# Pair layers: key copies and stores by context and own tokens, second unit's loads on ScalarE's queue

## The chip, the cores and the metric

One core of one Trainium2 chip. The metric is the device time of the whole program in microseconds, as the median of several executions.

## The reference, cut to what matters

Four attention layers run one after the other on x (4 batches of 256 tokens, 256 channels) with a context of the same shape. Layer 0 is a cross attention of two halves with an MLP, layer 2 a wide grouped attention. The change touches layers 1 and 3 alone, the pair layers:

```python
h = jnp.concatenate([x, latents], axis=1)               # x: the context, latents: the own tokens
q = (latents @ q_w + q_b).reshape(b, k_len, NH, DH)     # 16 heads of 16
kv = (h @ kv_w + kv_b).reshape(b, p + k_len, NH, DH, 2)
kmat, v = (kv[..., 0], kv[..., 1])
attn = jnp.einsum('bkhd,bnhd->bhkn', q, kmat) / DH      # 256 queries on 512 keys
attn = jnp.where(full_mask[:, None, None, :], attn, -jnp.inf)
attn = jax.nn.softmax(attn.astype(jnp.float32), axis=-1).astype(q.dtype)
attn_out = jnp.einsum('bhkn,bnhd->bkhd', attn, v).reshape(b, k_len, H)
```

The output projection, a norm and an MLP follow.

## The kernel before

The program is a row of stages. Each stage is a block in which SyncE, GpSimd, TensorE, ScalarE and VectorE run their own instruction lists, tied by semaphores, and ends with a barrier of all five. A pair layer (`pair_layer`, L2637) has three: projections (`pair_projections`, L1685, for layer 1; `scale_and_projections`, L2490, for layer 3, which first finishes layer 2), attention (`pair_attention`, L2048), and `project_and_mlp`.

**Projections.** Products are made from high and low float32r parts, three matmuls for one. `PairWork` lists 12 groups, each 128 output rows by 512 tokens, two batches: (is_k, m, src, half), where m is the block of eight heads (0, the *early* block, or 1, the *late* one), src 0 the context tokens and src 1 the own tokens. In both layers the order of the early block is: groups 0 and 1 context keys, 2 and 3 own keys, 4 and 5 queries. The late block follows as groups 6 to 11. For each group TensorE multiplies (`group`, L1630), ScalarE writes the high part with the bias (`high`, L1664), and VectorE writes the low part (`low`, L1669), which raises `qk_lo`. A PSUM bank is used again four groups later. Groups that read own tokens need their transposes (`turn`, L1623) split into parts by ScalarE and VectorE (`turned_high`, `turned_low`); groups of context keys read the context's parts, which lie ready. In layer 1 all four transposes come ahead of group 0. In layer 3 groups 0 and 1, then four tiles of values, come ahead of the transposes. Last come the values (`values`, `add_values`).

**Stacked operands.** The attention multiplies stacks of 48 rows, three sets of 16 for one head: (key high, query low), (key high, query high), (key low, query high). Row 48 holds the mask on the key side and ones on the query side; row 49 holds ones on the key side and the negated maxima on the query side. The 16 heads form four units of four heads; a unit's stacks lie in one of three slots. Since rows move between partitions, the stacks are filled by DMA:

- `fill_rows` (L1575): SyncE issues the six constant rows and waits for all.
- `copy_first_unit` (L1591): SyncE waits until `qk_lo` is 4 (`first_k`, both halves of the keys), issues 12 key copies, three for each head j, waits until it is 6 (`first_q`), issues 12 query copies, then waits for all 24 (`c.UNIT` is 24*16) and for the four stores. The stage can't end before that.
- `store_second_unit` (L1602): ScalarE, between `high` 7 and `high` 8, issues four DMAs which write the second unit's half of the early block to DRAM (`k_second`, `q_second`).

A key copy (L1520) moves 16 partitions with 8 KB each, a query copy (L1524) 16 partitions with 4 KB each:

```python
eng.dma_start(k_st[rows, a].bitcast(F32).rearrange("d b n -> d (b n)"),
              self.k[(0, 0, 1)[n]][at:at + c.HD].bitcast(F32).rearrange("d b s t -> d (b s t)")
```

**Attention.** There are 16 quads (unit, batch). A round works on the scores of one quad (`S`), the maxima of the one before (`M`), the shifted, transposed scores and exponentials of the one before that (`E`), and the value products of the next older one (`P`, `X`); the order on each engine is the text at L2056 to L2058. In a round SyncE waits for the negated maxima (`mx_out`) of a quad and issues two DMAs that put them into row 49 (L2115); the first `E` step of the next round waits for them (`row_in`, L2208). Behind them on the same queue: in rounds 0 and 1 (`first in (0, 1)`) the second unit's six key and six query loads from DRAM (`SecondUnit.load`, L1541), in rounds 2 to 5 the third unit's copies from the late block, six a round, in rounds 7 to 10 those of the fourth. The second unit is needed from round 4 on.

Of the kernel before, what the change touches and what calls it, by code (L numbers as in the profile page):

```python
# [5 lines left out]
P = 128  # L6
# [1497 lines left out]
class HeadParts:  # L1504
# [6 lines left out]

    def load_head(self, c, eng, g, j, q_st, k_st, sem, kinds="kq"):


        a, half = divmod(j, 2)
        at = (4 * (g % 2) + j) * c.HD
        for n in range(3):
            rows = slice(half * c.HALF + n * c.HD, half * c.HALF + (n + 1) * c.HD)
            if "k" in kinds:
                eng.dma_start(k_st[rows, a].bitcast(F32).rearrange("d b n -> d (b n)"),  # L1520
                              self.k[(0, 0, 1)[n]][at:at + c.HD].bitcast(F32).rearrange("d b s t -> d (b s t)")
                              ).then_inc(sem, 16)
            if "q" in kinds:
                eng.dma_start(q_st[rows, a].bitcast(F32).rearrange("d b t -> d (b t)"),  # L1524
                              self.q[(1, 0, 0)[n]][at:at + c.HD].bitcast(F32)).then_inc(sem, 16)


class SecondUnit:
# [6 lines left out]
    def store(self, eng, parts, sem):  # L1535
        for part in range(2):
            eng.dma_start(self.k[part], parts.k[part][P // 2:P].bitcast(F32).rearrange("c b s t -> c (b s t)")
                          ).then_inc(sem, 16)
            eng.dma_start(self.q[part], parts.q[part][P // 2:P].bitcast(F32)).then_inc(sem, 16)
# [12 lines left out]
class PairWork:  # L1552
# [4 lines left out]
    def __init__(self, st, core, c, late, second_unit, q_st, k_st, v_st, z, turned, qk_ps, groups):  # L1557
# [9 lines left out]
        self.tiles = [(src, b) for src in range(2) for b in range(B)]  # L1567
        self.first_k = max(n for n, g in enumerate(groups) if g[0] and not g[1]) + 1
# [22 lines left out]
    def copy_first_unit(self, sp):  # L1591
        c, z = self.c, self.z
        sp.wait_ge(z.qk_lo, self.first_k)
        for j in range(4):
            self.early.load_head(c, sp, 0, j, self.q_st[:, 0], self.k_st[:, 0], z.first_in, "k")
        sp.wait_ge(z.qk_lo, self.first_q)
        for j in range(4):
            self.early.load_head(c, sp, 0, j, self.q_st[:, 0], self.k_st[:, 0], z.first_in, "q")
        sp.wait_ge(z.first_in, c.UNIT)
        sp.wait_ge(z.stored, 4 * 16)  # L1600

    def store_second_unit(self, act):  # L1602
        act.wait_ge(self.z.qk_lo, self.first_q)
        self.second_unit.store(act, self.early, self.z.stored)
# [80 lines left out]
def pair_projections(core, c, late, second_unit, q_st, k_st, v_st):  # L1685

    with core.stage(f"p{c.layer}") as st:
# [6 lines left out]
        with core.nc.Block() as block:  # L1694
# [11 lines left out]
            def _(pe):  # L1706
                for n in range(4):
                    work.turn(pe, n)
                for g in range(len(groups)):
                    work.group(pe, g)  # L1710
# [4 lines left out]
            @block.scalar  # L1715
            def _(act):
                for n in range(4):
                    work.turned_high(act, n)
                for g in range(len(groups)):
                    if g == work.first_q + 2:  # L1720
                        work.store_second_unit(act)
                    work.high(act, g)

            @block.vector
            def _(dve):
                for n in range(4):
                    work.turned_low(dve, n)
                for g in range(len(groups)):
# [319 lines left out]
def pair_attention(core, c, weights, a_tok, late, second_unit, o_all, q_st, k_st, v_st):  # L2048
# [22 lines left out]
    with core.stage(f"s{L}") as st:  # L2071
# [15 lines left out]
        with nc.Block() as block:  # L2087
# [8 lines left out]
            def _(sp):  # L2096
# [12 lines left out]
                def body(first, second, third, fourth):  # L2109
# [8 lines left out]
                    if first in (0, 1):  # L2118
                        second_unit.load(c, sp, first == 0, slots[1][first == 0], unit_in[0])
# [14 lines left out]
            def _(act):  # L2134
                def body(first, second, third, fourth):
                    for kind, n in act_steps:
# [6 lines left out]
                        elif kind == "O" and fourth is not None:  # L2143
                            act.wait_ge(z.o_done, fourth + 1)
                            wait(act, z.x_done, fourth)
                            nc.scalar.activation(oT[:], o_ps, ACT.Copy).then_inc(z.o_out, 1)
                rounds(body)
# [342 lines left out]
def scale_and_projections(core, shared, before, c, gamma, beta, late, second_unit, q_st, k_st, v_st):  # L2490

    nc, ins, x, HT = core.nc, core.ins, core.x, TT // 2
    with core.stage(f"p{c.layer}") as st:
# [12 lines left out]
        with nc.Block() as block:  # L2506
# [39 lines left out]
            def _(act):  # L2546
# [17 lines left out]
                for g in range(2, len(groups)):  # L2564
                    if g == work.first_q + 2:
                        work.store_second_unit(act)
# [136 lines left out]
```

## Time and profile before

| | |
|---|---|
| median of 3 runs | 1305.93 us (1305.92 to 1308.3) |
| the profiled execution's own time | 1308.49 us |
| its span, first to last instruction | 1306.7 us |
| TensorE busy | 1211.3 us, 93% of the span |
| VectorE busy | 968.6 us, 74% |
| ScalarE busy | 736.1 us, 56% |
| GpSimd busy | 507.3 us, 39% |
| mean granted TensorE clock | 0.958 |
| projections of layer 1, attention of layer 1 begins | 714.20, 749.83 us |
| projections of layer 3, attention of layer 3 begins | 1071 (with layer 2's last part), 1124.18 us |

Times in the rows are microseconds from the span's start; a row gives start, duration, engine, line, operation, output<-inputs, shapes, a count where equal neighbours are merged, and in brackets how long the engine had been idle and what ended it. PE is TensorE, DVE VectorE, ACT ScalarE, SPq and ACTq the DMA issues of SyncE's and ScalarE's queues (their duration is that of the issue, not of the transfer). A release by PEq with the line of a stage's block is the barrier between two stages.

### The profile page before, as it was taken

The page shows a single profiled execution, that of the slowest core. Times are in us where ns is not written, and L with a number is a line of the kernel's source. Part 1 is how long each engine was busy: PE and PEld are TensorE (multiplying, and loading weights), DVE is VectorE, ACT ScalarE, POOL GpSimd, SP SyncE. Part 2 cuts the span into 40 slices and gives each one's busy share as a digit, 9 for nine tenths or more (in the row PEclk, how much of TensorE's full clock was granted, in tenths as well). Part 3 has the DMA queues.
Part 4 walks back from the last instruction along what each step waited for, and adds up shares of the span by engine and source line. Part 5 has one row for each costly group of instructions (what it writes and reads, how often), then busy time and mean ns, then how long its engine had stood idle before and what let it go on. Part 6 is the DMA issues. An engine that isn't in the chain of part 4 may idle for free. (4 is left out here: it accounts for less than half of the span.)

```text
span 1306.7 us, 27356 instructions
## 1 busy us (share of the span) xinstructions
PE 1211.3 (93%) x9144; PEld 1000.9 (77%) x9144; DVE 968.6 (74%) x2179; ACT 736.1 (56%) x1670; POOL 507.3 (39%) x670
## 2 busy tenths in 40 slices
PE   5999999999799999999889879999899999499989
PEld 4999999999699999999769735558677778255578
DVE  5878787887788788778785468947488876589474
ACT  5665655766466656567662237764166664077651
POOL 4645455444474454554041000122299970001040
PEclk9999999999899999999989959999999999589899
DMA  5210011010211101110030697220384003876021
GB/s 176 58 34 15 27 32 32 24 32 1 101 34 34 33 9 32 32 32 8 1 101 2 129 106 87 41 83 25 89 197 85 2 10 72 127 81 83 2 69 33
DMA packets 56534, 70.90 MB, mean 54 GB/s; under 512 B 6864, under 2 KB 47572, under 8 KB 54104
## 3 DMA queue, kind: packets, MB, share of 16 engines
q1 hardware_dynamic: 54832, 65.83, 24.7%
q10 hardware_dynamic: 1600, 3.76, 1.0%
q8 instruction: 57, 0.93, 0.3%
q14 instruction: 45, 0.37, 0.1%
HBM read 46.79 MB, written 8.13 MB: 42 GB/s over the span
## 5 line engine op out<-in xcount | busy, mean ns | idle before, releaser
L932 ACT ACTIVATE a_prob<-a_s_ps,a_negmax 128x257 f32<-128x257 f32 x256 | 119.0, 476 | 92.8 <-DVE a_negmax L1014 92.8
L2156 DVE TENSOR_REDUCE s_mx<-s_s_ps 128x2 f32<-128x1024 f32 x128 | 152.0, 1211 | 18.3 <-PE s_s_ps L2201 17.9
L2141 ACT ACTIVATE s_probT<-s_st_ps 128x512 f32<-128x512 f32 x256 | 132.2, 606 | 57.7 <-PE s_st_ps L2215 55.4
L873 POOL TENSOR_TENSOR x_v_hi<-a_v_sum,x_one 128x512 fp32r<-128x512 f32 x60 | 63.2, 1054 | 243.8 <-DVE a_v_sum L1003 243.8
L1938 POOL TENSOR_SCALAR s_below<-s_masked,s_mx 128x256 f32<-128x256 f32 x256 | 117.8, 480 | 4.0 <-DVE s_mx L1966 3.1
L1029 DVE TENSOR_TENSOR a_pT_lo<-a_t_ps,a_pT_hi 128x512 fp32r<-128x512 f32 x128 | 88.2, 689 | 37.2 <-ACT a_pT_hi L945 35.5
L1014 DVE TENSOR_REDUCE a_negmax<-a_s_ps 128x2 f32<-128x514 f32 x128 | 86.8, 688 | 23.0 <-PE a_s_ps L1075 22.9
L945 ACT ACTIVATE a_pT_hi<-a_t_ps 128x512 fp32r<-128x512 f32 x128 | 76.7, 599 | 46.7 <-PE a_t_ps L1129 43.1
L2278 POOL TENSOR_TENSOR a_k_high<-x_tok,parts_b_out 128x256 f32<-128x256 f32 x16 | 11.1, 731 | 229.3 <-DMA parts_b_out<-L_xattn_out_b 229.3
L1966 DVE CUSTOM_DVE_ANT_0 s_masked<-s_s_ps,l_mask 128x256 f32<-128x256 f32 x256 | 90.7, 420 | 4.5 <-PE s_s_ps L2003 4.5
L2201 PE MATMUL s_s_ps<-l_k_st,l_q_st 49*128 49x512 f32 x192 | 68.1, 546 | 22.2 <-PEq L2506 10.2
L1951 ACT ACTIVATE s_probT<-s_st_ps 128x512 f32<-128x512 f32 x128 | 69.7, 595 | 29.1 <-PE s_st_ps L2013 29.0
L1073 PE MATMUL a_s_ps<-x_k_hi,x_q_hi 128*128 128x258 f32 x256 | 74.5, 291 | 10.7 <-ACT a_prob L932 5.4
L948 ACT ACTIVATE a_oT_hi<-a_o_ps,a_hc 128x256 fp32r<-128x256 f32 x128 | 60.7, 474 | 37.0 <-PE a_o_ps L1075 29.7
L1073 PE MATMUL a_o_ps<-a_pT_hi,x_v_hi 128*128 128x256 f32 x256 | 81.1, 317 | 0.0
L1129 PE MATMUL a_t_ps<-ident,a_prob 128*128 128x128 f32 x512 | 77.2, 273 | 3.1 <-ACT a_prob L940 2.0
L2215 PE MATMUL s_st_ps<-l_q_st,l_k_st 50*128 50x256 f32 x384 | 70.0, 338 | 10.7 <-DMA l_q_st<-s_mxT 10.6
L875 POOL TENSOR_TENSOR x_v_lo<-a_v_sum,x_v_hi 128x512 fp32r<-128x512 f32 x60 | 77.4, 1290 | 4.7
L2215 PEld LDWEIGHTS s_st_ps<-l_q_st,l_k_st 50*128 50x128 f32 x384 | 48.3, 204 | 33.1 <-DMA l_q_st<-s_mxT 12.9
L1075 PE MATMUL a_s_ps<-x_k_hi,x_q_lo 128*128 128x258 f32 x256 | 72.6, 284 | 0.0
L1075 PE MATMUL a_g_ps<-a_wo_hi,a_oT_lo 128*128 128x256 f32 x256 | 72.6, 284 | 0.0
L1074 PE MATMUL a_s_ps<-x_k_lo,x_q_hi 128*128 128x258 f32 x256 | 72.6, 283 | 0.0
(348 smaller groups left out, 4039.3 us busy)
## 6 DMA issues: line engine op xcount, KB each, us to landing
a_wo_raw<-L_xattn_wo SPq DMA_DIRECT2D x16, 256.0 KB, 3.3
x_wqk_raw<-L_xattn_wq SPq DMA_DIRECT2D x31, 128.0 KB, 2.3
x_wqk_raw<-L_xattn_wk SPq DMA_DIRECT2D x31, 128.0 KB, 2.3
x_wv_raw<-L_xattn_wv SPq DMA_DIRECT2D x15, 256.0 KB, 3.1
l_k_st<-k_second SPq DMA_DIRECT2D x12, 256.0 KB, 9.8
l_k_st<-k_stack SPq DMA_DIRECT2D x16, 192.0 KB
l_q_st<-q_stack SPq DMA_DIRECT2D x12, 192.0 KB
x_vbias<-L_xattn_bias_v SPq DMA_DIRECT2D x2, 1024.0 KB, 6.5
```

Source lines behind the costliest of these rows:

```text
L875: nc.gpsimd.tensor_tensor(lo, raw, hi.bitcast(F32), ALU.subtract).then_inc(z.v_split, 1)
L932: nc.scalar.activation(prob[:, n % 2, qt, 0:NK], s_ps[:, n % 2, qt, 0:NK], ACT.Exp, bias=negmax[:, n % 2, qt:qt + 1], accum_out=den[:, n % ...
L1014: nc.vector.tensor_reduce(negmax[:, n % 2], s_ps[:, n % 2, :, 0:NK], AX.X, ALU.max, negate=True).then_inc(z.max_done, 1)
L1029: nc.vector.tensor_tensor(pT_lo[:, n % 2], t_ps[:], pT_hi[:, n % 2].bitcast(F32), ALU.subtract).then_inc(z.t_out, 1)
L1073: nc.tensor.matmul(out, a_hi, b_hi, start=start, stop=False)
L1075: return nc.tensor.matmul(out, a_lo, b_hi, start=False, stop=stop)
L1129: mm = nc.tensor.transpose(t_ps[:, at:at + P], prob[:, n % 2, qt, kt * P:(kt + 1) * P], core.ident[:])
L1938: nc.gpsimd.tensor_scalar(below[:, i % 2, h, qt], masked[:, i % 2, h, qt], -1.0, mx[:, i % 2, h, qt:qt + 1], ALU.mult, ALU.add).then_inc(z ...
L1966: nc.vector.tensor_tensor_reduce(out=masked[:, i % 2, h, qt], in0=s_ps[:, h, qt], in1=mask[:, i // NQ * QT + qt], scale=1.0, scalar=-3.0e3 ...
L2141: nc.scalar.activation(probT[:, third % 2, n // 4, n // 2 % 2, n % 2], st_ps[:, u % 3], ACT.Exp, scale=c.scale).then_inc(z.exp_done, 1)
L2156: nc.vector.tensor_reduce(mx[:, i % 2, qt, a::2], s_ps[:, n % 2], AX.X, ALU.max).then_inc(z.max_done, 1)
L2215: mm = nc.tensor.matmul(st_ps[:, u % 3, j * S:(j + 1) * S], k[:, a, kt * P:(kt + 1) * P], q[:, a], start=True, stop=True)
```

## The change

1. `copy_first_unit` copies keys by halves: when `qk_lo` is 2 (`context_k`) the context's 12 pieces (`load_key_half`: 16 partitions, four runs of 1 KB each), when it is 4 the own tokens' 12; queries as before; 36 DMAs for 24.
2. `store_second_unit` is called before each `high` and issues the context keys' two stores before `high` 4, the own keys' before `high` 6, the queries' before `high` 8; six DMAs for four.
3. In layer 1 groups 0 and 1 (and their `high` and `low`) go ahead of the transposes, as they do in layer 3.
4. The second unit's 12 loads are issued by ScalarE ahead of its first attention round, and no longer by SyncE in rounds 0 and 1.

```diff
--- before.py
+++ after.py
@@ -1509,6 +1509,15 @@
         self.k = [k_high if k_high and part == "hi" else st.sb(f"{name}_k_{part}", [P, B, 2, S], F32R)
                   for part in ("hi", "lo")]
 
+    def load_key_half(self, c, eng, j, src, k_st, sem):
+
+        a, half = divmod(j, 2)
+        tokens = slice(src * S, (src + 1) * S)
+        for n in range(3):
+            rows = slice(half * c.HALF + n * c.HD, half * c.HALF + (n + 1) * c.HD)
+            eng.dma_start(k_st[rows, a, :, tokens].bitcast(F32),
+                          self.k[(0, 0, 1)[n]][j * c.HD:(j + 1) * c.HD, :, src, :].bitcast(F32)).then_inc(sem, 16)
+
     def load_head(self, c, eng, g, j, q_st, k_st, sem, kinds="kq"):
 
 
@@ -1532,10 +1541,13 @@
         self.q = core.nc.dram_tensor(f"q_second{c.layer}", (2, P // 2, T), F32).ap()
         self.k = core.nc.dram_tensor(f"k_second{c.layer}", (2, P // 2, B * c.NK), F32).ap()
 
-    def store(self, eng, parts, sem):
+    def store_keys(self, eng, parts, src, sem):
         for part in range(2):
-            eng.dma_start(self.k[part], parts.k[part][P // 2:P].bitcast(F32).rearrange("c b s t -> c (b s t)")
-                          ).then_inc(sem, 16)
+            eng.dma_start(self.k[part].rearrange("c (b s t) -> c b s t", s=2, t=S)[:, :, src, :],
+                          parts.k[part][P // 2:P, :, src, :].bitcast(F32)).then_inc(sem, 16)
+
+    def store_queries(self, eng, parts, sem):
+        for part in range(2):
             eng.dma_start(self.q[part], parts.q[part][P // 2:P].bitcast(F32)).then_inc(sem, 16)
 
     def load(self, c, eng, is_k, dst, sem):
@@ -1565,6 +1577,7 @@
         self.bq, self.bk = columns(core, f"L{L}_xattn_q_b"), columns(core, f"L{L}_xattn_kv_b")
         self.chunks = [(kt, slice(half * 512, (half + 1) * 512)) for half in range(2) for kt in range(KT)]
         self.tiles = [(src, b) for src in range(2) for b in range(B)]
+        self.context_k = max(n for n, g in enumerate(groups) if g[0] and not g[1] and not g[2]) + 1
         self.first_k = max(n for n, g in enumerate(groups) if g[0] and not g[1]) + 1
         self.first_q = max(n for n, g in enumerate(groups) if not g[0] and not g[1]) + 1
 
@@ -1590,18 +1603,24 @@
 
     def copy_first_unit(self, sp):
         c, z = self.c, self.z
-        sp.wait_ge(z.qk_lo, self.first_k)
-        for j in range(4):
-            self.early.load_head(c, sp, 0, j, self.q_st[:, 0], self.k_st[:, 0], z.first_in, "k")
+        for src, count in enumerate((self.context_k, self.first_k)):
+            sp.wait_ge(z.qk_lo, count)
+            for j in range(4):
+                self.early.load_key_half(c, sp, j, src, self.k_st[:, 0], z.first_in)
         sp.wait_ge(z.qk_lo, self.first_q)
         for j in range(4):
             self.early.load_head(c, sp, 0, j, self.q_st[:, 0], self.k_st[:, 0], z.first_in, "q")
-        sp.wait_ge(z.first_in, c.UNIT)
-        sp.wait_ge(z.stored, 4 * 16)
-
-    def store_second_unit(self, act):
-        act.wait_ge(self.z.qk_lo, self.first_q)
-        self.second_unit.store(act, self.early, self.z.stored)
+        sp.wait_ge(z.first_in, 36 * 16)
+        sp.wait_ge(z.stored, 6 * 16)
+
+    def store_second_unit(self, act, g):
+        for src, count in enumerate((self.context_k, self.first_k)):
+            if g == count + 2:
+                act.wait_ge(self.z.qk_lo, count)
+                self.second_unit.store_keys(act, self.early, src, self.z.stored)
+        if g == self.first_q + 2:
+            act.wait_ge(self.z.qk_lo, self.first_q)
+            self.second_unit.store_queries(act, self.early, self.z.stored)
 
     def place(self, part, g):
         is_k, m, src, half = self.groups[g]
@@ -1704,9 +1723,11 @@
 
             @block.tensor
             def _(pe):
+                for g in range(2):
+                    work.group(pe, g)
                 for n in range(4):
                     work.turn(pe, n)
-                for g in range(len(groups)):
+                for g in range(2, len(groups)):
                     work.group(pe, g)
                 for n in range(8):
                     wait(pe, z.v_out, n - 3)
@@ -1714,18 +1735,21 @@
 
             @block.scalar
             def _(act):
+                for g in range(2):
+                    work.high(act, g)
                 for n in range(4):
                     work.turned_high(act, n)
-                for g in range(len(groups)):
-                    if g == work.first_q + 2:
-                        work.store_second_unit(act)
+                for g in range(2, len(groups)):
+                    work.store_second_unit(act, g)
                     work.high(act, g)
 
             @block.vector
             def _(dve):
+                for g in range(2):
+                    work.low(dve, g)
                 for n in range(4):
                     work.turned_low(dve, n)
-                for g in range(len(groups)):
+                for g in range(2, len(groups)):
                     work.low(dve, g)
                 for n in range(8):
                     work.add_values(dve, n)
@@ -2115,8 +2139,6 @@
                             sp.dma_start(slots[g % 3][0][m:m + 1, :, b].bitcast(F32),
                                          mxT[2 * half:2 * half + 2, second % 2].bitcast(F32)
                                          ).then_inc(row_in[second % 2], 16)
-                    if first in (0, 1):
-                        second_unit.load(c, sp, first == 0, slots[1][first == 0], unit_in[0])
                     if first is not None and 2 <= first <= 5:
                         late.load_head(c, sp, 2, first - 2, *slots[2], unit_in[1])
                     if first == 6:
@@ -2144,6 +2166,8 @@
                             act.wait_ge(z.o_done, fourth + 1)
                             wait(act, z.x_done, fourth)
                             nc.scalar.activation(oT[:], o_ps, ACT.Copy).then_inc(z.o_out, 1)
+                for is_k in (True, False):
+                    second_unit.load(c, act, is_k, slots[1][is_k], unit_in[0])
                 rounds(body)
 
             @block.vector
@@ -2562,8 +2586,7 @@
                 for n in range(4):
                     work.turned_high(act, n)
                 for g in range(2, len(groups)):
-                    if g == work.first_q + 2:
-                        work.store_second_unit(act)
+                    work.store_second_unit(act, g)
                     work.high(act, g)
 
             @block.vector
```

## Rows read from the trace of the kernel before

**Rows 1.** TensorE's timeline, layer 1: start us, us, engine, line, operation [idle before].
```profile
749.83 1.22 PE L2201 MATMUL s_s_ps<-l_k_st,l_q_st 49*128 49x512 f32 x4 [5.65 <-PEq L1694]
...
765.64 0.80 PE L2215 MATMUL s_st_ps<-l_q_st,l_k_st 50*128 50x256 f32 x4 [5.43 <-DMA l_q_st<-s_mxT]
```

**Rows 2.** TensorE's timeline, layer 3.
```profile
1124.18 1.22 PE L2201 MATMUL s_s_ps<-l_k_st,l_q_st 49*128 49x512 f32 x4 [10.17 <-PEq L2506]
...
1139.76 0.80 PE L2215 MATMUL s_st_ps<-l_q_st,l_k_st 50*128 50x256 f32 x4 [5.21 <-DMA l_q_st<-s_mxT]
```

**Rows 3.** Waits of SyncE's queue, whole run: us in total, times, longest.
```profile
SPq L1593 <- DVE p_early_k_lo L1671: 19.4, 2, 16.7
...
SPq L1694 <- DMA l_q_st<-p_early_q_hi: 1.6, 1, 1.6
...
SPq L1520 <- DMA l_k_st<-p_ones: 0.9, 1, 0.9
```

**Rows 4.** Timeline of SyncE's queue, layer 1.
```profile
724.21 1.18 SPq L1520 DMA_DIRECT2D l_k_st<-p_early_k_hi  x2
...
738.94 1.11 SPq L1524 DMA_DIRECT2D l_q_st<-p_early_q_lo  x1
...
746.45 1.22 SPq L1524 DMA_DIRECT2D l_q_st<-p_early_q_hi  x2
...
749.79 2.68 SPq L1548 DMA_DIRECT2D l_k_st<-k_second  x6
...
757.13 1.30 SPq L2115 DMA_DIRECT2D l_q_st<-s_mxT  x2
...
758.48 2.84 SPq L1548 DMA_DIRECT2D l_q_st<-q_second  x6
```

**Rows 5.** Timeline of SyncE's queue, layer 3: the last issue.
```profile
1120.80 1.22 SPq L1524 DMA_DIRECT2D l_q_st<-p_early_q_hi  x2
```

**Rows 6.** VectorE's timeline, layer 1.
```profile
715.50 2.48 DVE L1661 TENSOR_TENSOR p_x_lo<-p_turned,p_x_hi 128x512 fp32r<-128x512 f32 x4 [1.62 <-ACT p_x_hi L1656]
...
744.22 0.69 DVE L1680 TENSOR_TENSOR l_v_st<-p_turned,bv_row 128x512 f32<-128x512 f32 x1 [0.74 <-PE p_turned L1621]
```

**Rows 7.** VectorE's timeline, layer 3.
```profile
1087.55 0.74 DVE L1671 SCALAR_TENSOR_TENSOR p_early_k_lo<-p_t_ps,cols,p_early_k_hi 128x512 fp32r<-128x512 f32 x1
...
1098.04 0.75 DVE L1671 SCALAR_TENSOR_TENSOR p_early_k_lo<-p_t_ps,cols,p_early_k_hi 128x512 fp32r<-128x512 f32 x1 [0.95 <-ACT p_early_k_hi L1666]
...
1112.57 2.47 DVE L1680 TENSOR_TENSOR l_v_st<-p_y_ps,bv_row 128x512 f32<-128x512 f32 x4
```

**Rows 8.** DMA on SyncE's queue, packets, MB, share: 1082 to 1086, 740 to 744, 750 to 756.
```profile
q1 hardware_dynamic: 91, 0.05, 18.8%
...
q1 hardware_dynamic: 189, 0.45, 73.3%
...
q1 hardware_dynamic: 127, 0.78, 97.3%
```

**Rows 9.** DMA issues of 724 to 728, 728 to 732, 740 to 744: median us to landing.
```profile
l_k_st<-p_early_k_hi SPq DMA_DIRECT2D x4, 128.0 KB, 4.6
...
l_k_st<-p_early_k_hi SPq DMA_DIRECT2D x2, 128.0 KB, 5.7
...
l_q_st<-p_early_q_hi SPq DMA_DIRECT2D x4, 64.0 KB, 2.4
```

**Rows 10.** ScalarE's timeline and its queue's, layer 1.
```profile
728.74 2.75 ACTq L1537 DMA_DIRECT2D k_second<-p_early_k_lo  x1
...
749.79 1.28 ACT L2141 ACT_TABLE_LOAD   x1 [14.29 <-PEq L1694]
...
766.48 1.09 ACT L2141 ACTIVATE s_probT<-s_st_ps 128x512 f32<-128x512 f32 x2 [15.40 <-PE s_st_ps L2215]
```

**Rows 11.** Windows: us, busy times, granted clock (PEclk), DMA share, GB/s.
```profile
748.00:749.00 1.00, 0.00 (x0) 0.00 (x0) 0.00 (x0) 0.00 (x0) 0.00 (x0) 0.50 0.47 82
...
778.00:779.00 1.00, 1.00 (x10) 0.69 (x6) 0.03 (x1) 0.38 (x1) 0.00 (x0) 0.65 1.44 148
```

## The prediction

> **What bounds the kernel now.** TensorE is busy for most of the span, so I read where it stands still in the two pair layers (layers 1 and 3), since only they are touched. First TensorE's timeline. Attention of layer 1 begins at 749.83, after 5.65 us of idleness that end with the stage's closing barrier, and some ten microseconds on TensorE idles again, 5.43 us, for the DMA of the row of maxima, `l_q_st<-s_mxT` [rows 1]. Layer 3 shows the same two holes, 10.17 and 5.21 us [rows 2]. Together 26.5 us in 1306.7.
>
> What holds the barrier is in SyncE's queue (SPq), not in an engine. VectorE's last instruction of layer 1's projections ends at 744.91 [rows 6], but SPq issues the 24 copies of the first unit until 747.67 [rows 4] and then waits 1.6 us for the last to land [rows 3]. In layer 3 VectorE ends at 1115.04 [rows 7] and SPq at 1122.02 [rows 5].
>
> When could SPq begin? In layer 1 it waits 0.9 us for the DMA of the row of ones, *after* the own keys are ready [rows 3]: the constant rows, not the keys, set the start 724.2. In layer 3 it sits 16.7 us waiting for the own keys [rows 3], though the context keys were finished at 1088.29 and the own keys at 1098.79 [rows 7]. The constant rows were issued by 1098.8-16.7 = 1082.1 and landed, at layer 1's 2.7+0.9 = 3.6 us after issue (19.4 less 16.7, and 0.9 [rows 3]), near 1085.7. So layer 3 has a free stretch from 1088.3, layer 1 has none: its context keys would be ready earlier too, but the rows of ones still land at 724.1.
>
> **Term 1, copies by halves.** 12 key copies of 128 KB become 24 of 64 KB; the 12 query copies stay: 36 issues for 24. Old prices: keys 724.21 to 738.94 = 14.7 us for 12, or 1.23 each; queries 738.94 to 747.67 = 8.7 us for 12, the undisturbed ones 0.61 (two in 1.22 [rows 4]), with a step to the next about 0.63. A new half copy has the bytes (64 KB), the 16 source partitions and the 16 target partitions of a query copy, but pieces of 1 KB instead of 4 KB. Ends for one half: below, 0.61, the issue itself; above, 0.96, four times the 0.24 us that a 1 KB packet took while the rows of ones were filled (18.8% of 16 engines over 4 us = 12.0 us for 0.05 MB, some 50 pieces [rows 8]). That row writes one single partition, the query copies write sixteen, as the halves do, so I take 0.63. The DMA engines then have room: query copies alone fill 73% of them [rows 8]. The stores of ScalarE fall into the same stretch; beside them the old queue needed 23.5 us (724.21 to 747.67) where its keys at the rate of the query copies (0.45 MB in 4 us [rows 8], 1.16 us for 128 KB) and its queries, 12x1.16+12x0.63 = 21.5, would do. Of these 2.0 us I charge 1.4, since the stores now come in smaller pieces and partly earlier; ends 0 and 2.0.
> Layer 1: 36x0.63+1.4 = 24.1 for 23.5: **+0.6 us** (ends: -0.9 without disturbance, +8.5 at 0.96 each).
> Layer 3: context halves from 1088.3 take 12x0.63 = 7.6 and end at 1095.9, before the own keys at 1098.8, so they cost nothing; their cover is 10.5 us. From 1098.9: 24x0.63+1.4 = 16.5, end of issue 1115.4 instead of 1122.0: **-6.6 us**. Late next: VectorE's end, 1115.04; it is passed by little, so -8.7 (start right after VectorE, some 0.4 us of barrier) is the best case, and at 0.96 per half only -1.6 remains (12x0.33 = 4.0 for the own keys, 12x0.96-10.5 = 1.0 for the context).
>
> **Term 2, TensorE's, ScalarE's and VectorE's order in layer 1.** Context groups 0 and 1 go ahead of the transposes. The own tokens' groups then wait for two transposed chunks, whose lows (2.48 us for four [rows 6]) now stand behind two key lows: at most 1.5+1.2 = 2.7 us later, I reckon 1.2. Cover: VectorE ends 4.9 us before attention begins [rows 1, 6]. Cost zero while SPq is last; the queries are ready long before their turn on SPq.
>
> **Term 3, stores by halves.** 4 DMAs on ScalarE's queue become 6, of which two come ahead of group 4's copy, two ahead of 6, two ahead of 8. Behind them stand the highs that free TensorE's banks. Now the third of the four stores takes 2.75 us to issue [rows 10], and nothing came late, because the next groups had their banks. Two half stores are half the bytes of what the old four moved two by two, so a pair costs 1 to 2 us, and a bank is wanted four groups on. Zero; above, 2 us of TensorE delay per layer, which in layer 1 the cover takes, and in layer 3 the 2.2 us that are left between VectorE's end with its barrier (1115.4) and the new start (1117.6).
>
> **Term 4, the second unit's loads.** SPq now issues six key loads first, 2.68 us [rows 4], 1.5 MB that run at 0.78 MB in 6 us and fill the engines to 97% [rows 8]: 12 us of backlog. The row of maxima is issued at 757.13 into the same queue and its wait ends at 765.64, 8.5 us later [rows 1, 4]; the six query loads follow. After: all twelve are on ScalarE's queue from the start, the row is alone in SPq's. A lone 64 KB copy lands 2.4 us after issue; copies of SPq landed in 4.6 us by themselves and 5.7 with ScalarE's stores beside them [rows 9], 1.1 more. Ends for the row: not later than now (gain 0), or landing as a lone copy, 757.7+2.4 = 760.1, which frees the whole 5.4 us. The row meets a denser queue on the other side than those copies did, so I take 2.4 plus twice 1.1 = 4.6 behind the second row's issue at 757.8: 762.4 instead of 765.6, a gain of **3.2 us per layer**. Given back: the third unit's copies (from the third round on) follow on SPq's queue 3.2 us earlier, into loads that still run until 1.5+0.75 MB at 0.13 MB per us = 17.3 us after the start; the row of the round after then queues behind them. Ends: 0 and all of the 3.2. I charge **0.8 us** per layer, a quarter, since only that round meets both. Twice -2.4 = **-4.8 us**.
> ScalarE pays twelve issues: 2.68+2.84 = 5.5 us [rows 4], against a first exponential now 16.65 us after the start [rows 1, 10], and about 13 after it in the new one. Free, if the queue takes twelve without halting.
>
> **The clock.** Attention starts at the low level, 1.2 GHz (granted 0.50 at 748), and gets 2.4 GHz back at 778.3 inside the first dense run of value products (0.65 in that microsecond) [rows 11]. I let it do the same again, at the same point of the rounds: no term.
>
> **Sum.** +0.6-6.6-4.8 = -10.8 us on the profiled execution (1308.49, of which 1306.7 is span): 1297.7. It stands 2.56 over the median of the runs, 1305.93; the same difference there gives **1295.1 us**. 0.2%, 2.6 us, is about what a measurement of this kernel can tell from no change.
>
> **Rivals.**
> *A. The row comes no earlier* (1299.9, chance 0.18). The engines are 97% busy with loads that began 7 us before; if what decides is the engine's backlog and not the queue, the row waits as now. For: the copies under stores landed later, not unchanged. Against: they were only 1.1 us later beside 1.5 MB from the other queue. Then +0.6-6.6 = -6.0: 1299.9.
> The Trainium skill ("DMA: Bandwidth & Descriptors", "Issuing engines are not separate DMA queues") speaks for this rival: DMAs of all issuers interleave on the same 16 engines, and another issuer saves only sequencer time. By that rule I would drop term 4 and say 1299.9. Its section "Queues, rings and completion order" has each engine take turns between queues packet by packet, which by itself would give the forecast.
> *B. ScalarE halts in issuing* (1303.9, chance 0.10). Its third store took 2.75 us [rows 10]. If twelve loads are taken only as fast as they run, 17.3 us, the first exponential follows the table load (1.28 us [rows 10]) at 18.6 after the start instead of 16.65: +2.0 a layer in place of -2.4. Sum -6.0+4.0 = -2.0: 1303.9. Against: SPq put six query loads in 2.84 us behind six key loads of which a part still ran [rows 4].
> *C. The 1 KB pieces make the copies slow* (1309.9, chance 0.03). The price is the row-of-ones packet, 0.24x4 = 0.96 and its closing packet, some 1.0 us a half: layer 1 gets 24x0.37 = 8.9 later, layer 3 12x0.37+12x1.0-10.5 = 5.9. Sum -10.8+14.8 = +4.0: 1309.9. It decides from about 0.97 us per half on (the sum then passes +2.6). Against: sixteen partitions share the load here, where the rows of ones fill one.
> *D. More than forecast* (about 1292, chance 0.12): rows land as lone copies, nothing is given back: -6.0-10.4 = -16.4, or 1289.5; half of that, 1292.
> The forecast itself has 0.57. Range: B's and C's far ends left out, 1289.5 to 1301.5. Faster by over 0.2%: forecast, A, D and a third of B, 0.90; within: the rest of B, 0.07; slower: C, 0.03.
>
> **What would show it.** Right: in layer 3 twelve copies issued from about 1088 to 1096, attention beginning 6 to 7 us earlier, some 4 us after the last value product; in layer 1 the gap still 4 to 6 us with SPq's 36 issues about 0.63 apart; TensorE's wait for `s_mxT` near 2 us instead of 5.4 and 5.2; ScalarE's twelve issues in under 7 us. Wrong: half copies well over 0.63 (C), the `s_mxT` wait unchanged (A), an exponential waiting for ScalarE's own issues (B), a VectorE or TensorE end later than SPq's in layer 3, or rounds two to six longer by what the first one gained.

## The result: slower by 10 us

| | before | after |
|---|---|---|
| median, both kernels on one chip (5 runs each) | 1306.56 us (1305.92 to 1308.3) | 1318.51 us (1317.11 to 1321.86) |
| the profiled execution, its span | 1308.49, 1306.7 us | 1318.51, 1316.7 us |
| mean granted TensorE clock | 0.958 | 0.954 |

The ratio after to before is 1.008, 95% interval 1.0052 to 1.0109. Forecast were 1295.1 us and a gain of 10.8; the profiled executions lie 10.0 the other way, the medians 12.0, and the sums below take the profiled pair apart. Busy times hardly moved (TensorE 1213.5 for 1211.3 us), so it is waiting again. TensorE's timeline of the changed kernel, the lines that answer to [rows 1, 2]; the first of each pair is the beginning of the attention, the second the first score step that needs the row of maxima:

```profile
754.46 1.22 PE L2225 MATMUL s_s_ps<-l_k_st,l_q_st 49*128 49x512 f32 x4 [8.60 <-PEq L1713]
...
775.21 0.80 PE L2239 MATMUL s_st_ps<-l_q_st,l_k_st 50*128 50x256 f32 x4 [10.38 <-DMA l_q_st<-s_mxT]
...
1131.19 1.22 PE L2225 MATMUL s_s_ps<-l_k_st,l_q_st 49*128 49x512 f32 x4 [5.75 <-PEq L2530]
...
1151.41 0.80 PE L2239 MATMUL s_st_ps<-l_q_st,l_k_st 50*128 50x256 f32 x4 [9.84 <-DMA l_q_st<-s_mxT]
```

Where before 5.4 and 5.2 us of waiting for the row stood, there are 10.4 and 9.8. Layer 1's attention starts 4.6 us later than before; layer 3's hole before the attention shrank from 10.17 to 5.75. The stages' first TensorE instructions, in layers 1 and 3, give the lengths:

```profile
714.54 0.47 PE L1638 MATMUL p_qk_ps<-c_hi,parts_w_parts 128*128 128x512 f32 x1 [0.78 <-PEq L1427]
...
1082.56 1.94 PE L2321 MATMUL p_t_ps<-ident,parts_o_all 128*128 128x128 f32 x16 [0.82 <-PEq L1928]
```

In order of time: stage of layer 1 begins +0.3; its projections take 39.9 instead of 35.6 (**+4.3**); from the attention's start to the row 20.75 instead of 15.81 (**+4.9**); between there and layer 3's stage +1.8 that I can't assign; layer 3's projections 48.6 instead of 53.0 (**-4.4**); its row 20.2 instead of 15.6 (**+4.6**); the rest -1.6. Sum +10.0.

**Layer 1's copies.** SyncE's queue, the first twelve issues and the last:

```profile
724.54 2.28 SPq L1518 DMA_DIRECT2D l_k_st<-p_early_k_hi  x2
726.86 1.17 SPq L1518 DMA_DIRECT2D l_k_st<-p_early_k_lo  x1
728.07 2.69 SPq L1518 DMA_DIRECT2D l_k_st<-p_early_k_hi  x2
730.81 1.29 SPq L1518 DMA_DIRECT2D l_k_st<-p_early_k_lo  x1
732.14 2.29 SPq L1518 DMA_DIRECT2D l_k_st<-p_early_k_hi  x2
734.47 0.60 SPq L1518 DMA_DIRECT2D l_k_st<-p_early_k_lo  x1
735.11 1.23 SPq L1518 DMA_DIRECT2D l_k_st<-p_early_k_hi  x2
736.39 0.59 SPq L1518 DMA_DIRECT2D l_k_st<-p_early_k_lo  x1
...
751.03 1.22 SPq L1533 DMA_DIRECT2D l_q_st<-p_early_q_hi  x2
```

The last issue ends at 752.25, 27.7 us after the first; before it was 23.5 [rows 4]. Two kinds of step are seen: from 735.11 on 0.63 to 0.64 each, and nine issues, 724.54 to 735.11, that took 10.6 us instead of 9x0.635 = 5.7. In these ten microseconds ScalarE's six stores run (issued 723.41 to 730.05); 724 to 728 on the DMA view:

```profile
q10 hardware_dynamic: 657, 0.64, 78.0%
q1 hardware_dynamic: 80, 0.07, 5.0%
```

(q10 is ScalarE's queue, q1 SyncE's: packets, MB, share of the 16 engines.) SyncE's copies got 5% while the stores drained.

**Layer 3's copies.** The context's twelve, the beginning of the own tokens', and the last issue:

```profile
1099.77 1.36 SPq L1518 DMA_DIRECT2D l_k_st<-p_early_k_hi  x2
...
1107.17 0.60 SPq L1518 DMA_DIRECT2D l_k_st<-p_early_k_lo  x1
1110.22 1.89 SPq L1518 DMA_DIRECT2D l_k_st<-p_early_k_hi  x2
...
1113.34 2.67 SPq L1518 DMA_DIRECT2D l_k_st<-p_early_k_hi  x2
...
1121.43 0.59 SPq L1533 DMA_DIRECT2D l_q_st<-p_early_q_lo  x1
...
1127.78 1.23 SPq L1533 DMA_DIRECT2D l_q_st<-p_early_q_hi  x2
```

The context's pieces fit into the free stretch (8.0 us for twelve); the own tokens' again took 11.2 us instead of 7.6, beside the stores.

**The row of maxima.** ScalarE and its queue as layer 1's attention begins:

```profile
754.43 2.73 ACTq L1560 DMA_DIRECT2D l_k_st<-k_second  x6
757.18 3.59 ACTq L1560 DMA_DIRECT2D l_q_st<-q_second  x6
760.81 1.28 ACT L2163 ACT_TABLE_LOAD   x1 [25.73 <-issue]
776.04 1.08 ACT L2163 ACTIVATE s_probT<-s_st_ps 128x512 f32<-128x512 f32 x2 [13.95 <-PE s_st_ps L2239]
```

Twelve issues in 6.3 us, ScalarE ready at 762.1, the first exponential at 776.04 waits for TensorE. SyncE issued the rows from 761.75 on, into a queue that held nothing else. The DMA view of 766 to 774 and, below it, of 772 to 773:

```profile
q10 hardware_dynamic: 316, 0.97, 99.2%
q1 hardware_dynamic: 8, 0.00, 0.5%
...
q10 hardware_dynamic: 48, 0.13, 104.5%
q1 hardware_dynamic: 2, 0.00, 1.4%
```

All eight packets of SyncE's queue moved after 772 (two in this microsecond, six in the next), with the last of the twelve loads. The view counts a million bytes as 1 MB: the 2.25 MB of the twelve loads are 2.36 MB there, at the 0.13 MB per us seen here 18.1 us, and 754.4+18.1 = 772.5.

### The profile page after: what moved, and what is told of

The parts are those of the page before. It is cut to its first block and busy times, and to the rows that moved or that the text cites. A ratio compares the mean times of both kernels' runs of the same rounds, so it can differ in the third digit from the quotient of the medians.

```text
span 1316.7 us, 27384 instructions
## 1 busy us (share of the span) xinstructions
PE 1213.5 (92%) x9144; PEld 1002.0 (76%) x9144; DVE 969.0 (74%) x2179; ACT 737.9 (56%) x1670; POOL 507.9 (39%) x670
## 5 line engine op out<-in xcount | busy, mean ns | idle before, releaser
L1029 DVE TENSOR_TENSOR a_pT_lo<-a_t_ps,a_pT_hi 128x512 fp32r<-128x512 f32 x128 | 88.3, 690 | 37.3 <-ACT a_pT_hi L945 35.5
L2239 PE MATMUL s_st_ps<-l_q_st,l_k_st 50*128 50x256 f32 x384 | 70.3, 338 | 20.2 <-DMA l_q_st<-s_mxT 20.2
L1073 PE MATMUL a_g_ps<-a_wo_hi,a_oT_hi 128*128 128x256 f32 x256 | 72.6, 284 | 0.0
```

The source lines that it names most:

```text
L1029: nc.vector.tensor_tensor(pT_lo[:, n % 2], t_ps[:], pT_hi[:, n % 2].bitcast(F32), ALU.subtract).then_inc(z.t_out, 1)
L1073: nc.tensor.matmul(out, a_hi, b_hi, start=start, stop=False)
L2239: mm = nc.tensor.matmul(st_ps[:, u % 3, j * S:(j + 1) * S], k[:, a, kt * P:(kt + 1) * P], q[:, a], start=True, stop=True)
```

## Experiments

The expectations name theories, some by a letter. **I** (order of issue): a row of maxima lands when the bytes issued ahead of it have gone, on whatever queue they stand; before, six loads stood ahead of it (1.5 MB), after, twelve (2.25 MB). Its rivals: each queue gets its turn, and the delay is the density of the traffic or a path that SyncE and ScalarE share. **S** (stores): copies of SyncE's queue are held while ScalarE's stores drain, and since issuing is the bound, a hold is never made up.

### e1 and e2: the two halves of the change

e1 is the changed kernel with the loads back on SyncE's queue (rounds 0 and 1); e2 is the kernel before with term 4 alone:

```diff
-                    if first in (0, 1):
-                        second_unit.load(c, sp, first == 0, slots[1][first == 0], unit_in[0])
...
+                for is_k in (True, False):
+                    second_unit.load(c, act, is_k, slots[1][is_k], unit_in[0])
                 rounds(body)
```

> The changed kernel with the second unit's loads back on SyncE's queue in rounds 0 and 1; copies and stores by halves and layer 1's order stay. Theory I (the row of maxima moves only after every transfer issued ahead of it, whichever queue they stand in): the wait for the row falls from 10.4 and 9.8 us back to 5.4 and 5.2; what is left is +4.3 us of layer 1's projections and -4.4 us of layer 3's, so 1306.5, within 2 us of the kernel before. Theory II (the halves cost the ten microseconds, and the longer row wait only fills time that something else would take): it stays at 1314 or more.

> The kernel before with only one part of the change, the twelve loads issued by ScalarE ahead of its rounds. Theory I: the row waits for 2.25 MB of loads instead of 1.5 MB, 5 us more a layer, so about 1316.5; the projections are those of before. Theory II: within 2 us of the kernel before, 1306.5.

e1: ratio 1.0018 (0.9997 to 1.0038). e2: 1.0108 (1.0059 to 1.0156). TensorE in e2, layers 1 and 3:

```profile
750.48 1.22 PE L2201 MATMUL s_s_ps<-l_k_st,l_q_st 49*128 49x512 f32 x4 [5.64 <-PEq L1694]
...
771.30 0.80 PE L2215 MATMUL s_st_ps<-l_q_st,l_k_st 50*128 50x256 f32 x4 [10.44 <-DMA l_q_st<-s_mxT]
...
1132.03 1.22 PE L2201 MATMUL s_s_ps<-l_k_st,l_q_st 49*128 49x512 f32 x4 [10.73 <-PEq L2506]
...
1151.92 0.80 PE L2215 MATMUL s_st_ps<-l_q_st,l_k_st 50*128 50x256 f32 x4 [9.51 <-DMA l_q_st<-s_mxT]
```

All of the loss that can be told from noise is in the loads' new place; the copies as changed come out at little or nothing (e1's interval ends at +5 us).

### e3: only the six key loads on ScalarE's queue

```diff
-                for is_k in (True, False):
-                    second_unit.load(c, act, is_k, slots[1][is_k], unit_in[0])
+                second_unit.load(c, act, True, slots[1][1], unit_in[0])
...
+                    if first == 1:
+                        second_unit.load(c, sp, False, slots[1][0], unit_in[0])
```

> The changed kernel with only the six key loads issued by ScalarE at the start; the six query loads by SyncE in round 1 behind the row, as before. Theory I: the row waits for 1.5 MB, whoever issued it: the first shifted step 15.8 us after the attention's start, as before, wait 5.2 to 5.5 us, time as e1. Theory III (the engines take turns between the two queues, but the turns are long or ScalarE's queue comes first while it has much queued): with half as many DMAs in front the row lands sooner than in order, a wait under 4 us, time 2 to 4 us under e1.

Ratio 1.0029 (1.0008 to 1.005), and the row (layer 1):

```profile
769.85 0.80 PE L2240 MATMUL s_st_ps<-l_q_st,l_k_st 50*128 50x256 f32 x4 [5.27 <-DMA l_q_st<-s_mxT]
```

With 1.5 MB ahead of the row TensorE goes on 15.7 us after the attention's start, whether they stand on ScalarE's queue (e3) or on SyncE's own (15.8 before, 15.7 in e1). What counts is the amount issued ahead.

### e5: the rows from a third queue

The changed kernel, its rows of maxima issued by GpSimd:

```diff
-                            sp.dma_start(slots[g % 3][0][m:m + 1, :, b].bitcast(F32),
...
+                for i in range(c.quads):
+                    g, b = batch(i)
+                    pool.wait_ge(z.mx_out, i + 1)
+                    for half in range(2):
+                        m = half * HALF + c.MAX_ROW
+                        pool.dma_start(slots[g % 3][0][m:m + 1, :, b].bitcast(F32),
```

> The changed kernel, its twelve loads still on ScalarE's queue at the start, but the rows of maxima issued by GpSimd, whose queue is neither SyncE's nor ScalarE's. If what the row stands behind is the path of descriptors that SyncE's and ScalarE's queues share, it lands within some 4 us of its issue: TensorE's waits of 10.4 and 9.8 us shrink to 3 us or less and the time is 1306 or less. If it is the backlog of the 16 engines themselves, it moves only behind the loads again: waits near 10 us, time 1316 to 1320.

1.0159 (1.0138 to 1.018), 1328.6 us, slower than either theory had it. The first row's wait in layer 1, on TensorE's timeline:

```profile
773.82 0.80 PE L2242 MATMUL s_st_ps<-l_q_st,l_k_st 50*128 50x256 f32 x4 [10.80 <-DMA l_q_st<-s_mxT]
```

The DMA view of 755 to 775, with the row's size and its time from issue to landing:

```profile
l_q_st<-s_mxT POOLq DMA_DIRECT2D x2, 2.0 KB, 13.0
```

A third queue is served no sooner: 10.8 and, in layer 3, 10.1 us. So it is not a path that only SyncE and ScalarE share. In later rounds TensorE now waits for rows too, up to 1.6 us at a time, some 6 us in all; the rest of the loss was not taken apart.

### e4: less in front of the row

The kernel before with its loads spaced: three key loads in round 0, three in round 1, six query loads in round 2, the third unit one round later.

```diff
                     if first in (0, 1):
-                        second_unit.load(c, sp, first == 0, slots[1][first == 0], unit_in[0])
-                    if first is not None and 2 <= first <= 5:
+                        second_unit.load(c, sp, True, slots[1][1], unit_in[0], (first,))
+                    if first == 2:
+                        second_unit.load(c, sp, False, slots[1][0], unit_in[0])
+                    if first is not None and 3 <= first <= 6:
```

> The kernel before with the second unit's loads spaced on SyncE's queue: three key loads in round 0 (0.75 MB, 6 us, done before the row is issued at 7.3 us), three in round 1 behind the row, the six query loads in round 2, the third unit's copies one round later (3 to 6). Theory I: the first row lands some 2.5 us after its issue, the 5.4 and 5.2 us waits fall to 1 us or less; later rows stand behind 6 us of transfers in rounds of 5.9 us and may wait 1 us: -4 us a layer, 1298.5. Theory II (backlog of the engines decides, and total bytes are the same): no more than 2 us gained, 1304.5 or more.

A miss: 1.0048 (1.003 to 1.0065), slower. The first row, behind three loads, costs no wait any more, as theory I has it: issued at 756.14, it is used at 759.02. The first line below is the *second* row, which stands behind the other three; then come the first value products and what happens at the third unit:

```profile
767.02 0.80 PE L2217 MATMUL s_st_ps<-l_q_st,l_k_st 50*128 50x256 f32 x4 [2.43 <-DMA l_q_st<-s_mxT]
...
770.27 2.63 PE L2230 MATMUL s_ox_ps<-s_probT,l_v_st 128*17 128x256 f32 x32
...
800.91 0.50 PE L2203 MATMUL s_s_ps<-s_k_third,parts_w_parts 49*128 49x512 f32 x2 [2.88 <-DMA parts_w_parts<-l_q_st]
...
804.10 3.62 PE L2230 MATMUL s_ox_ps<-s_probT,l_v_st 128*17 128x256 f32 x32
```

The first value products begin 21.4 us after the attention's start (before 24.8: 774.66 less 749.83), a gain of 3.4. But the third unit's copies come a round later and stand, six of them, ahead of its constant rows in the same round: TensorE waits 2.88 us for those rows until 800.91, and the value products behind take 3.62 us instead of the 1.92 that they took in the rounds before (794.63 in this trace). The windows show what followed that stop (the column behind the five busy times is the granted clock); the last line is the kernel before, over the same stretch:

```profile
798.00:801.00 3.00, 0.12 (x3) 0.09 (x2) 0.66 (x3) 0.84 (x2) 0.00 (x0) 1.00 0.20 26
...
804.00:806.00 2.00, 2.00 (x21) 0.83 (x24) 1.41 (x2) 0.49 (x2) 0.00 (x0) 0.50 0.98 100
...
795.00:812.00 17.00, 17.00 (x174) 9.93 (x166) 15.31 (x22) 12.85 (x27) 0.00 (x0) 1.00 0.60 69
```

From 804 to 808 TensorE, wholly busy, has 1.2 GHz again, where the kernel before kept 2.4 from 795 to 812. Layer 3 waits the same way (2.45 and 2.71 us). As I read it, this gives the 3.4 us back and more; no run changed the constant rows alone.

### e6: the stores moved behind the last `high`

```diff
                 for g in range(2, len(groups)):
-                    work.store_second_unit(act, g)
                     work.high(act, g)
+                for g in range(2, len(groups)):
+                    work.store_second_unit(act, g)
```

It stands on top of e1, in both layers.

> The copies-only kernel (e1) with ScalarE's six stores at the end of its list, after the last high. Theory S (SyncE issues one half copy in 0.64 us and is the bound; beside the stores it is held, and a held issue is never made up): the first nine copies of layer 1, 10.6 us in the changed kernel, take 5.8; ten or so later ones are held instead; last issue of layer 1 within 1.5 us of e1's, time within 2 us of e1's 1308.5. Theory P (pieces of 1 KB are slow at the beginning, by the rows or the keys themselves, whatever the stores do): the first nine still take 9 us or more and the stores cost their own time later, 1312 or more.

1.0029 (1.0016 to 1.0042). SyncE's queue in layer 1:

```profile
721.23 1.38 SPq L1518 DMA_DIRECT2D l_k_st<-p_early_k_hi  x2
...
726.49 0.60 SPq L1518 DMA_DIRECT2D l_k_st<-p_early_k_lo  x1
...
731.56 1.88 SPq L1518 DMA_DIRECT2D l_k_st<-p_early_k_hi  x2
...
734.88 2.82 SPq L1518 DMA_DIRECT2D l_k_st<-p_early_k_hi  x2
...
747.83 1.22 SPq L1533 DMA_DIRECT2D l_q_st<-p_early_q_hi  x2
```

ScalarE's queue there, the first and the last of its six stores:

```profile
731.17 0.60 ACTq L1546 DMA_DIRECT2D k_second<-p_early_k_hi  x1
...
736.35 1.36 ACTq L1551 DMA_DIRECT2D q_second<-p_early_q_lo  x1
```

The first nine copies now take 5.9 us (721.23 to 727.13), and the held ones are nearly all from 731 on, where the stores are (one pair, at 729.04, took 1.83 us for 1.22 ahead of them). The 36 take 27.8 us as before: the hold moves with the stores and is never made up.

### e9 and e10: halves in layer 3 alone, the new order alone

e9 is the kernel before with items 1 and 2 of the change in layer 3 only; layer 1 keeps whole keys and the old order, with its six stores ahead of `high` 8. e10 is the kernel before with item 3 alone.

```diff
+        if c.layer == 3:
+            for src, count in enumerate((self.context_k, self.first_k)):
...
+        else:
+            sp.wait_ge(z.qk_lo, self.first_k)
+            for j in range(4):
+                self.early.load_head(c, sp, 0, j, self.q_st[:, 0], self.k_st[:, 0], z.first_in, "k")
```

> The kernel before with halves in layer 3 alone (copies and stores as in the changed kernel there); layer 1 copies whole keys with its six stores ahead of high 8, in the old order of groups; the loads stay on SyncE's queue in rounds 0 and 1. If the part of the change that pays is the free stretch of layer 3, and the part that costs is the number of issues in layer 1, the gain seen in layer 3 of the run with the copies alone (-4 us) is alone here and the 4 us of layer 1 are gone: ratio 0.997 (996 to 0.998 in thousandths), layer 1's attention begins within 1 us of [rows 1], layer 3's stage is 4 us shorter up to the attention. Rival (the halves lengthen something else, later in the layers, so that the copies alone come out at +2): the ratio stays at 1.000 or above.

> The kernel before with term 2 alone: in layer 1 groups 0 and 1 ahead of the transposes on TensorE, ScalarE and VectorE. My theory (SyncE's queue is last and begins at the rows of ones, not at the keys): ratio 1.000 within 0.001, attention of layer 1 within 0.5 us of [rows 1]. Rival (the own keys or the queries come late to SyncE's queue, or the stores late to ScalarE's): up to +2 us, ratio 1.0015.

e9: 0.9986 (0.9969 to 1.0003); e10: 0.9994 (0.9977 to 1.0011); each scattered over 9 us on that chip, the kernel before over 7.6. The totals tell neither from 1; the stages do:

| projections, first instruction to attention, us | layer 1 | layer 3 |
|---|---|---|
| whole keys: before, e2, e4, e10 | 35.6, 35.6, 35.7, 35.5 | 53.0, 52.0, 52.1, 51.6 |
| halves: after, e1, e3, e5, e6 | 39.9, 39.3, 39.4, 39.8, 40.0 | 48.6, 47.4, 48.6, 47.2, 49.4 |
| e9: whole in layer 1, halves in layer 3 | 34.1 | 49.0 |
| e7, e8 (below): the same, shared queries, other places of the stores | 34.8, 33.1 | 45.3, 45.3 |

Each is one execution; equal code differs by up to 0.7 us in layer 1 and 1.4 in layer 3. By the means, halves cost 39.7-35.6 = 4.1 us in layer 1 and bring 52.2-48.2 = 4.0 in layer 3. The order costs nothing (e10, 35.5).

### e7 and e8: what the readings suggest

e7: loads as before; layer 1 whole keys, layer 3 halves; and since issuing on one queue is the bound, the last six query copies are issued by ScalarE after its last `high`; the keys' stores go ahead of `high` 7, in layer 3 the context's ahead of the transposes.

```diff
         sp.wait_ge(z.qk_lo, self.first_q)
-        for j in range(4):
-            self.early.load_head(c, sp, 0, j, self.q_st[:, 0], self.k_st[:, 0], z.first_in, "q")
+        self.copy_queries(sp, range(2))
...
                     work.high(act, g)
+                work.copy_queries(act, range(2, 4))
```

e8: on top of it the second unit's loads spaced as three, three and six, the keys first, and the third unit's constant rows fetched in round 2 instead of 6, in 1 KB pieces, so that the rows that were late in e4 are early; the third unit's copies come one round later, as in e4.

> Second unit's loads as before on SyncE's queue. Layer 1: whole key copies as before, the last six query copies issued by ScalarE after its last high. Layer 3: key copies by halves, context stores before the transposes' highs, last six query copies by ScalarE. If issue is the bound of the projections' end: layer 1's last issue goes from 747.7 to 744 or so and attention starts 3 us earlier; layer 3's last issue goes to about 1115 on the old clock, attention 7 us earlier; 1296.5. If the transfers are the bound (all queues in one order), layer 1 gains under 1 us and layer 3 as in the changed kernel 4.5 us: 1301.

> e7 and the second unit's loads spaced: three key loads in round 0, two key and one query load in round 1, the rest in round 2, the constant rows split into pieces of 1 KB in round 2, the third unit's copies in rounds 3 to 6. e4 showed the first wait gone, 2.4 us at the second row and then 2.9 us for the constant rows at round 8 with the clock lost again. Here 3.5 to 4.5 us a layer under e7: 1289. If the third unit's copies are still late at round 8, nothing or a loss beside e7.

e7: 1300.07 us, 0.9929 (0.99 to 0.9958). e8: **1295.39 us, 0.9904 (0.9882 to 0.9926)**, faster than both kernels. Whether e8 beats e7 is not settled: its intervals overlap e7's, and the 4.7 us between the medians are under the 7 to 9 us forecast. TensorE in e7, layers 1 and 3:

```profile
747.66 0.73 PE L2230 MATMUL s_s_ps<-l_k_st,l_q_st 49*128 49x512 f32 x4 [1.05 <-PEq L1720]
...
1115.05 1.16 PE L2230 MATMUL s_s_ps<-l_k_st,l_q_st 49*128 49x512 f32 x4 [2.69 <-PEq L2535]
```

The hole ahead of layer 1's attention is down to 1.05 us, but the stage is only 0.8 us shorter than before (34.8 for 35.6), where 3 was expected: VectorE's last value product is the bound now, and it ends at 747.34, 34.5 us into the stage, where before it ended 30.7 us in. ScalarE issues its four stores of keys, 724.48 to 730.34, ahead of `high` 7, and VectorE's low parts wait for that (the row puts its gap down to TensorE, but the last of these issues ends 0.05 us ahead of it):

```profile
730.39 0.69 ACT L1692 ACTIVATE a_k_high<-p_qk_ps,cols 128x512 fp32r<-128x512 f32 x1 [5.24 <-PE p_qk_ps L1647]
```

e9 does no worse in layer 1 (34.1) without shared queries. The gain of e7 is in layer 3, 7.7 us (45.3 for 53.0), 3.7 of them beyond e9's halves; how much of that is the second queue and how much the stores' new places was not taken apart. In e8 the first row costs no wait, and the later rows' waits are 1.82 us in layer 1 and 1.32 and 1.92 in layer 3, for 5.8 and 5.3 of the first row in e7; TensorE no longer waits for the constant rows:

```profile
765.72 0.80 PE L2248 MATMUL s_st_ps<-l_q_st,l_k_st 50*128 50x256 f32 x4 [1.82 <-DMA l_q_st<-s_mxT]
...
1128.11 0.80 PE L2248 MATMUL s_st_ps<-l_q_st,l_k_st 50*128 50x256 f32 x4 [1.32 <-DMA l_q_st<-s_mxT]
...
1138.61 0.80 PE L2248 MATMUL s_st_ps<-l_q_st,l_k_st 50*128 50x256 f32 x4 [1.92 <-DMA l_q_st<-s_mxT]
```

## Why the prediction was wrong

**Term 4 failed, in its sign: +9.5 us for -4.8.** The step is "the row is alone in SPq's ... so I take 2.4 plus twice 1.1". It priced the row by copies issued *beside* stores, and let the other queue only thin out its turns. It took SyncE's own queue for what held the row before (six loads ahead on the same queue), and so moving them away looked like a gain. e3 shows that moving them changes nothing, and e2 that six more of them ahead of the row cost 5.0 and 4.3 us. The bound "not later than now (gain 0)" was false too: the query loads, which stood behind the row on SyncE's queue, stand ahead of it on ScalarE's, and they are 0.75 MB, some 6 us at 0.13 MB per us, which my own sum of 17.3 us contained (18.1 in the view's own MB). The term left out what the moved step is moved *ahead* of. The price of "1.1 more" was poor as well: the 4.6 us for copies "by themselves" are the median of 724 to 728, and stores run from 727.25; of these copies the first two landed in 3.7 us, those of 728 to 729 in 5.8 and 6.8.

Rival A named the right cause, the engines' backlog, and drew the wrong amount from it: "the row waits as now" forgot the same 0.75 MB. By the Trainium skill ("DMA: Bandwidth & Descriptors", "Issuing engines are not separate DMA queues") all issuers share the same 16 engines, and the runs agree (5.3 us of wait on either queue, 10.8 from a third). Its section "Queues, rings and completion order", from which the forecast got its support, has an engine drain a whole packet, by the page typically 9 to 17 descriptors and at most 64, before it turns to another queue. Turns fine enough for the forecast are not what is seen: from the row's issue at 761.75 to 772 the DMA view counts 311 packets of its own kind (single pieces of up to 8 KB) on ScalarE's queue, 19 for each of the 16 engines, and none of the row's. Whether very long turns would look the same no run here tells.

**Term 1, layer 1: +4.3 for +0.6.** The price of a half, 0.63, was right to a hundredth, and rival C (slow 1 KB pieces) falls. Mis-sized was the disturbance by the stores: 4.9 us (10.6 less 5.7) for 1.4, though its end was put at 2.0. The old trace hid it: as I read it (no run took it apart), whole keys are bound by the transfer (1.16 of 1.23 us), so that a hold partly replaces waiting that is due anyway, while halves are bound by the issue and lose all of it. By the sum, 36x0.635+4.9 = 27.8, measured 27.7.

**Term 1, layer 3: -4.4 for -6.6.** The mechanism was right (e9 repeats it, 49.0 for 53.0): context pieces issued in the free stretch at 0.67 each, attention nearer to the last value product. Off is the same disturbance, 11.2 us for twelve instead of 7.6: 3.6 for the 1.4 charged.

**Terms 2 and 3** came out at nothing, as forecast: e10 shows it for the order; the six stores took 0.47 to 0.64 us each to issue and held up no `high` that mattered. Placed together ahead of `high` 7, the stores do (e7, layer 1).

**Rival B** falls: twelve issues in 6.3 us, not 17.3. **Rival D** falls with the forecast. **The clock** was no term by itself: 0.50 from the attention's start to the first dense value products in both kernels. But these come later now, so a longer stretch runs at 1.2 GHz (in layer 1 until 32.5 us after the attention's start for 28.5); that and the 1.8 us between the layers were not taken apart.

With the measured lengths of both stages and both rows in place of mine the sum is +4.3-4.4+4.9+4.6 = +9.4, of the +10.0 seen.

**Open.** Where the order between queues is kept is not shown, only that three queues obey it for a small transfer behind large loads. Nor was a large copy tried behind another queue's loads. Whole keys with six late stores (e9, 34.1) beat the old four by 1.5 us in layer 1: the 24 copies are issued in 21.9 us (722.00 to 743.88) for 23.5; why, was not followed up.

## What to carry to other kernels

Here a small transfer that an engine waits for landed after the large loads that were issued ahead of it, on whichever of three queues it stood: count the backlog in MB, over all queues, at the moment of its issue, and issue bulk loads in portions behind it. Another queue brought the row nothing. For copies of 0.64 us an issue a second queue may pay where issuing is the bound (e7, layer 3), but issues placed ahead of ScalarE's own work delayed what waits for that work (e7, layer 1). Copies split in two paid only where a free stretch took the added issues.

## What the hardware showed that I had not expected

- A 2 KB row issued at 761.75 moved its first packet after 772, behind 2.25 MB of another queue; from GpSimd's queue it landed after 13.0 us.
- Beside another queue's stores the *issue* of a copy grows from 0.64 us to 1.2, on average of nine, and up to 2.82 us for two (e6); the hold moved when the stores were moved.
- 64 KB in 1 KB pieces on sixteen partitions is no dearer to issue than in 4 KB pieces (0.63 us) and lands in the same 2.4 us [rows 9]; after, from 740 to 744:

```profile
l_k_st<-p_early_k_hi SPq DMA_DIRECT2D x5, 64.0 KB, 2.4
```
